# Turning the adjacency in 32x32 squares on VectorE instead of on TensorE

## The chip, the cores and the metric

The kernel runs on one core of one Trainium2 chip. Its time is the device time of one launch in microseconds (us). A core has TensorE (PE; PEld are its weight loads), VectorE (DVE), ScalarE (ACT), GpSimd (POOL) and SyncE (SP), each with its own instruction queue, and 16 DMA engines. SBUF has 128 partitions, PSUM eight banks. Engines wait for one another only by semaphores.

## The reference

A batch of 2048, each with 50 nodes of 32 features. Every sample makes its own two adjacency matrices of 50 x 50, and one gated step is taken with them; what comes behind (batch norm, layer norm, attention pooling over the nodes) is stage three, which the change does not touch.

```python
fusion = x.reshape(b, n * d)                                   # 2048 x 1600
adj = jnp.einsum('bn,tnm->btm', fusion, masker_param) + masker_bias   # 2048 x 2 x 2500
adj = jax.nn.relu(adj).reshape(b, t, n, n)
adj = adj / (adj.sum(axis=-1, keepdims=True) + 1e-06)
m = jnp.einsum('btnd,de->btne', h, weight[i])
m = jnp.einsum('btnm,btmd->btnd', adj, m)
gates = m @ w_ih.T + b_ih + h @ w_hh.T + b_hh
...
```

## The kernel before

The batch lies in 16 tiles of 128 samples. All matrices are fp32; where it matters a value is split into a high and a low part (`_hi`, `_lo`) and a product is made of three.

**Stage one** makes the adjacency. Samples are the partitions of the result; the 5000 columns (2 x 50 rows n of 50 columns m) are cut into 10 groups of 10 rows (`GN`), 500 columns (`GW`). A *window* is one tile and one group: 38 products of 128 x 500 into one of two PSUM banks (`window`, L430; products at L445). Eight windows with the same weights are an *iteration*; 10 iterations are a *block* of eight tiles, and there are two blocks: 160 windows. For each window, one window later:

- ScalarE applies relu from PSUM into `u` (L307).
- VectorE normalises: sum of each row, plus epsilon, reciprocal, product into `an` (`normalise`, L357 to L365).
- TensorE turns `an`, four transposes by a product with the identity, 125 columns each, behind the fourth pair of K blocks of the *next* window (`transposes`, L421, L427, called where `i == T_AT`).
- ScalarE evacuates the turned tile from PSUM into `at` (L313), waiting for the store before last of the same buffer.
- SyncE stores `at` to the scratch `adjT` in HBM (`store_tile`, L201): rows (n, m), columns samples.

In the last window of an iteration ScalarE also casts the next weights to `w_hi` (L288) and VectorE subtracts to `w_lo` (L294); TensorE's first window of the next iteration waits for these. In the first iteration (and the last of block one) the x tiles are split in the same way, one tile a window (L259 to L272); their loads stand in SyncE's queue behind the store of the window before. The order within each engine's queue is written out by hand.

**Stage two** takes tiles one by one, in eight rounds of 16 samples. `load_adj` (L128) brings a tile's adjacency with m in the partitions: 50 partitions for each half of 64 samples, in pieces of 64 samples (256 bytes). `aggregate` (L766) multiplies for each sample its adjacency (moving, 100 columns picked with a step) with its x (stationary), two samples at once for the two halves; then come the gates (L793, L799), the turn of h (on VectorE in 32x32 squares, L708, and on TensorE, L810), and the statistics. SyncE loads a tile's adjacency and x two tiles ahead, when the slot's products are done. The gates of round 6 of an even tile wait for the next tile's three loads (`adj_loaded[1]`, 48 = 3 x 16), behind the products of round 7. The first tile's inputs are loaded in stage one's last iteration; those of the second tile (tile 1) when stage two starts.

Of the kernel before, what the change touches and what calls it, by code (L numbers as in the profile page):

```python
# [17 lines left out]
fp32 = mybir.dt.float32  # L18
# [24 lines left out]
MPAD = 64  # L43
RK = 125
AK = GW // RK
assert AK * RK == GW and AK * P == 512
# [6 lines left out]
T_AT = 3  # L53
# [91 lines left out]
def stage1(nc, place, psum, ins, adjT, shared):  # L145
    xT, W, ident_d = ins["xT"], ins["W"], ins["ident"]
    with ExitStack() as ctx:  # L147
# [9 lines left out]
        ident = sb("ident_sb", [P, P])  # L157
# [6 lines left out]
        x_loaded, ident_loaded = [sem("x_loaded0"), sem("x_loaded1")], sem("ident_loaded")  # L164
# [4 lines left out]
        tr_done, at_ready = sem("tr_done"), sem("at_ready")  # L169
# [8 lines left out]

        def tr_out(c2):

            return psum[0:RK, (2 + c2) * BANK:(3 + c2) * BANK]

# [3 lines left out]
        def _(sp):  # L186
# [25 lines left out]
            sp.dma_start(ident[:, :], ident_d).then_inc(ident_loaded, 16)  # L212
# [89 lines left out]
        def _(act):  # L302
# [17 lines left out]
            for blk in range(BLOCKS):  # L320
                for it, group in p1_iters(act, blk):
                    static = isinstance(it, int)
                    for w in range(BLK):
# [10 lines left out]
                        if split:  # L334
                            for i in range(0, T_AT + 1):
                                split_w_hi(act, i, it + 1)
                        if not (static and it == 0 and w == 0):
                            evacuate(c - 1, (w - 1) % 2, start=static and it == 0 and w <= 2)
                        if split:
                            for i in range(T_AT + 1, NU):  # L340
# [9 lines left out]
            evacuate(c, 1)  # L350
# [1142 lines left out]
```

## Time and profile before

| | us |
|---|---|
| median of 3 runs (lowest, highest) | 2220.93 (2220.83, 2222.51) |
| profiled execution, its own time | 2223.07 |
| span in the profile, first to last instruction | 2221.3 |
| PE busy / DVE busy / ACT busy in the span | 2167.1 / 1088.7 / 956.7 |
| mean granted clock of TensorE, of full speed | 0.988 |
| DMA packets, bytes; packets under 512 B | 341777, 264.48 MB; 169340 |

How to read the rows below. In a windows view each row is a stretch: its length, then for each engine the busy time and the number of instructions, then the granted clock of TensorE (1.00 is 2.4 GHz, 0.50 is 1.2 GHz), the mean busy share of the 16 DMA engines and the GB/s that they moved. In a timeline each row is one instruction or a run of like ones: start, duration, engine, line, output and inputs, count (x16), and in brackets the idle time before it and who ended it. Durations of matmuls overlap, so their pace is read from starts. SPq rows are DMA issues: the duration is how long the issue held the queue, not the transfer.

### The profile page before, as it was taken

The numbers are of one execution on the slowest core, as the hardware profiler recorded it, in microseconds if no ns is written. First come the engines' busy times: TensorE is split into PE (matmuls) and PEld (weight loads), VectorE is DVE, ScalarE is ACT, GpSimd is POOL, SyncE is SP. The second block draws the span as 40 slices with busy tenths as digits, with TensorE's granted clock in tenths as the row PEclk, the third lists the DMA queues.
The fourth block names the chain that finished last, engine by engine and source line by source line (L and its number), as shares of the span: only waits on it lengthen the run. The fifth ranks groups of instructions, "written<-read, shape, count | busy, mean of one in ns | idle before, by whom it ended". The sixth has DMA issues, their size and how long they took to land. (4 is left out here: it accounts for less than half of the span.)

```text
span 2221.3 us, 34738 instructions
## 1 busy us (share of the span) xinstructions
PE 2167.1 (98%) x12334; PEld 1721.3 (77%) x12334; DVE 1088.7 (49%) x2209; ACT 956.7 (43%) x1631; POOL 67.3 (3%) x68
## 2 busy tenths in 40 slices
PE   8999999999999999999999999989999999996898
PEld 7888888888888888888888888867777777775333
DVE  4432233323333433233322333238888888888667
ACT  4321222212223322122221222158888888895862
POOL 0000000000000000000000000010101111010000
PEclk9999999999999999999999999989999999998999
DMA  6412222122205321222212221457776676774660
GB/s 220 157 43 77 92 92 82 41 93 92 92 28 193 125 95 37 85 92 92 74 48 95 92 91 29 118 125 185 189 204 177 193 194 184 197 205 152 191 183 8
DMA packets 341777, 264.48 MB, mean 119 GB/s; under 512 B 169340, under 2 KB 303004, under 8 KB 339996
## 3 DMA queue, kind: packets, MB, share of 16 engines
q1 hardware_dynamic: 323580, 226.12, 34.7%
q10 hardware_dynamic: 18144, 37.69, 5.2%
q8 instruction: 29, 0.48, 0.1%
q14 instruction: 24, 0.20, 0.0%
HBM read 196.08 MB, written 67.70 MB: 119 GB/s over the span
## 5 line engine op out<-in xcount | busy, mean ns | idle before, releaser
L445 PE MATMUL psum<-w_hi,x_lo 128*128 128x500 f32 x2080 | 821.0, 395 | 8.0 <-DVE w_lo L294 8.0
L445 PE MATMUL psum<-w_lo,x_hi 128*128 128x500 f32 (+1 forms) x2080 | 808.3, 389 | 0.0
L445 PE MATMUL psum<-w_hi,x_hi 128*128 128x500 f32 x1920 | 744.0, 388 | 0.0
L357 DVE TENSOR_REDUCE rows<-u 128x10 f32<-128x500 f32 x160 | 107.5, 672 | 887.0 <-ACT u L307 886.4
L445 PEld LDWEIGHTS psum<-w_hi,x_lo 128*128 128x128 f32 x2080 | 391.5, 188 | 82.3 <-issue 8.0
L445 PEld LDWEIGHTS psum<-w_lo,x_hi 128*128 128x128 f32 (+1 forms) x2080 | 391.9, 188 | 72.2
L445 PEld LDWEIGHTS psum<-w_hi,x_hi 128*128 128x128 f32 x1920 | 360.9, 188 | 73.0
L313 ACT COPY at<-psum 125x512 f32<-125x512 f32 x160 | 93.5, 584 | 676.6 <-PE psum L427 676.6
L307 ACT ACTIVATE u<-psum 128x500 f32<-128x500 f32 x160 | 93.8, 586 | 341.3 <-PE psum L445 341.3
L766 PE MATMUL psum<-adj_sb,xs_sb 100*64 100x100 f32 x2048 | 200.6, 350 | 1.6 <-PEq L147 1.6
L766 PEld LDWEIGHTS psum<-adj_sb,xs_sb 100*64 100x64 f32 x2048 | 144.4, 149 | 45.6 <-issue 35.3
L629 ACT ACTIVATE r_gate<-psum,bias 64x400 f32<-64x400 f32 x256 | 151.0, 590 | 22.9 <-PE psum L793 20.8
L288 ACT CAST w_hi<-w_raw 128x1000 fp32r<-128x1000 f32 (+1 forms) x140 | 136.1, 972 | 46.0 <-PE psum L445 44.5
L294 DVE TENSOR_TENSOR w_lo<-w_raw,w_hi 128x1000 fp32r<-128x1000 f32 x120 | 144.0, 1200 | 23.6 <-ACT w_hi L288 15.9
L634 ACT ACTIVATE psum<-psum,bias 64x400 f32<-64x400 f32 x256 | 142.3, 556 | 14.0 <-DVE hG L689 7.1
L746 POOL TENSOR_TENSOR xg_lo<-xg_sb,xg_hi 128x400 fp32r<-128x400 f32 x64 | 67.1, 1051 | 1926.3 <-ACT xg_hi L595 1926.3
L365 DVE TENSOR_TENSOR an<-u,rows 128x500 f32<-128x500 f32 x160 | 108.6, 679 | 6.9
L697 DVE BATCH_NORM_STATS2 stats<-hC 128x128 f32 (+1 forms) x400 | 88.4, 282 | 47.1 <-ACT hC L607 46.6
L427 PEld LDWEIGHTS psum<-ident_sb,an 128*125 128x125 f32 x640 | 94.9, 188 | 16.4 <-DVE an L365 3.0
L427 PE MATMUL psum<-ident_sb,an 128*125 128x128 f32 x640 | 96.5, 274 | 3.4 <-DVE an L365 3.4
L674 DVE SCALAR_TENSOR_TENSOR n_in<-psum,bias,r_gate 128x400 f32<-128x400 f32 x128 | 79.5, 621 | 14.1 <-PE psum L799 13.6
L1127 DVE SCALAR_TENSOR_TENSOR pr<-h,nmu_sb,psum 128x512 f32<-128x512 f32 x100 | 70.0, 742 | 27.9 <-PE psum L1308 26.7
(169 smaller groups left out, 2135.1 us busy)
## 6 DMA issues: line engine op xcount, KB each, us to landing
w_raw<-W SPq DMA_DIRECT2D x140, 500.0 KB, 7.9
adjT<-at SPq DMA_DIRECT2D x160, 250.0 KB
adj_sb<-adjT SPq DMA_DIRECT2D x32, 1250.0 KB
xs_sb<-xz SPq DMA_DIRECT2D x16, 1600.0 KB
hF<-hC ACTq DMA_DIRECT2D x96, 256.0 KB, 6.3
h<-hF SPq DMA_DIRECT2D x64, 256.0 KB, 4.2
xg_sb<-xg ACTq DMA_DIRECT2D x14, 800.0 KB, 8.0
h<-hF SPq DMA_DIRECT2D x48, 192.0 KB, 3.4
```

The costliest lines, as they stand in the source:

```text
L288: nc.scalar.copy(w_hi[:, k0:k1, :], w_raw[:, k0:k1, :]).then_inc(w_hi_ready, 1)
L294: nc.vector.tensor_tensor(w_lo[:, k0:k1, :], w_raw[:, k0:k1, :], w_hi[:, k0:k1, :].bitcast(fp32), ALU.subtract).then_inc(w_ready, 1)
L307: nc.scalar.activation(u[:, c2].rearrange("p n m -> p (n m)"), mm_out(c2), ACT.Relu).then_inc(u_ready, 1)
L313: nc.scalar.copy(at[:, c2].rearrange("p k b -> p (k b)"), tr_out(c2)).then_inc(at_ready, 1)
L357: nc.vector.tensor_reduce(rows[:, 0], u[:, c2], AX.X, ALU.add).then_inc(dve_step, 1)
L365: nc.vector.tensor_tensor(an[:, c2], u[:, c2], rows[:, 2].unsqueeze(2).to_broadcast([P, GN, N]), ALU.mult).then_inc(an_ready, 1)
L427: last = nc.tensor.transpose(tr_out(c2)[:, k * P:(k + 1) * P], flat[:, k * RK:(k + 1) * RK], ident[:, :])
L445: last = nc.tensor.matmul(mm_out(w % 2), a[0:r, w, k, :], b[0:r, k, :], start=k == 0 and n == 0, stop=k == KF and n == 1)
L629: last = nc.scalar.activation(r_gate[half], rz_bank(pair)[half], ACT.Sigmoid, bias=bias[half, R_G:R_G + 1])
L634: last = nc.scalar.activation(z_bank[half], rz_bank(pair)[other], ACT.Sigmoid, bias=bias[other, Z_G:Z_G + 1])
L697: last = nc.vector.bn_stats(stats[:, bass.ds(tile, 1), c, :].rearrange("p i v -> p (i v)"), hC[:, c, :])
L766: last = nc.tensor.matmul(out_[SH * i:SH * i + SH, :, gi], xs[r][:, b, :], adj[r][:, :, b], start=True, stop=True)
```

## The change

VectorE turns each normalised tile right behind `normalise` with one transpose instruction that turns every square of 32 x 32 by itself. `an` becomes one buffer with each row of 50 padded to 64 (`MPAD`), the padding cleared once at the start; `at` holds, in partition 32i+m', for k (m = 32k + m') and n, the 32 samples of group i. The next normalisation waits for the turn of the one before; the turn waits for the store two windows back. TensorE's transposes, ScalarE's evacuation, the identity's load and two PSUM banks go from stage one. The scratch has the order `[tile, k, (i m'), n, s]`, 3.28 MB a tile instead of 2.56; a store is 128 partitions x 2 pieces of 1280 bytes. A tile is loaded in four transfers instead of two, for each half one of the 32 rows with k=0 and one of the 18 rows left, in pieces of 100 x 32 words (12.8 KB); the waits for them go from 48 to 80. The products of `aggregate` pick their moving columns with a step of 32 words instead of 64.

```diff
 def load_adj(sp, shared, adjT, tile, r=0):
     for half in range(2):
-        sp.dma_start(shared.adj[r][N * half:N * half + N], adjT[tile, :, SH * half:SH * half + SH].rearrange("(c m) s -> m c s", m=N)
-                     ).then_inc(shared.adj_loaded[r], 16)
+        for k in range(MB):
+            m0, m1 = TB * k, min(TB * k + TB, N)
+            sp.dma_start(shared.adj[r][N * half + m0:N * half + m1].rearrange("p i c s -> p i (c s)"),
+                         adjT[tile, k, SH * half:SH * half + SH].rearrange("(i m) c s -> m i (c s)", m=TB)[0:m1 - m0]
+                         ).then_inc(shared.adj_loaded[r], 16)
...
-        an = sb("an", [P, 2, GN, N])
+        an = sb("an", [P, GN, MPAD])
-        at = sb("at", [RK, 2, AK, P])
+        at = sb("at", [P, 2, MB, GN, TB])
...
-                sp.dma_start(adjT[tile, bass.ds(group * GW, GW), :].rearrange("(k p) b -> p k b", p=RK),
-                             at[:, c2]).then_inc(at_stored[c2], 16)
+                sp.dma_start(adjT[tile, :, :, bass.ds(group * GN, GN), :].rearrange("k p n s -> p k (n s)"),
+                             at[:, c2].rearrange("p k n s -> p k (n s)")).then_inc(at_stored[c2], 16)
...
-            def evacuate(c, c2, start=False):
-                act.wait_ge(tr_done, c + 1)
-                if not start:
-                    act.wait_ge(at_stored[c2], 8 * (c - c2))
-                nc.scalar.copy(at[:, c2].rearrange("p k b -> p (k b)"), tr_out(c2)).then_inc(at_ready, 1)
...
+            def turn_squares(c, c2, start=False):
+                dve.wait_ge(an_ready, c + 1)
+                if start:
+                    dve.wait_ge(an_cleared, 1)
+                else:
+                    dve.wait_ge(at_stored[c2], 8 * (c - c2))
+                nc.vector.transpose(at[:, c2], an[:].rearrange("p n (k s) -> p k n s", s=TB)).then_inc(at_ready, 1)
...
+            nc.vector.memset(an[:, :, N:MPAD], 0.0).then_inc(an_cleared, 1)
...
                         if not (static and it == 0 and w == 0):
-                            normalise(c - 1, (w - 1) % 2, start=static and it == 0 and w <= 2)
+                            normalise(c - 1, (w - 1) % 2, first=static and it == 0 and w == 1)
+                            turn_squares(c - 1, (w - 1) % 2, start=static and it == 0 and w <= 2)
...
-            def transposes(c, c2, start=False):
-                pe.wait_ge(an_ready, c + 1)
-                if not start:
-                    pe.wait_ge(at_ready, c - 1)
-                flat = an[:, c2].rearrange("p n m -> p (n m)")
-                for k in range(AK):
-                    last = nc.tensor.transpose(tr_out(c2)[:, k * P:(k + 1) * P], flat[:, k * RK:(k + 1) * RK], ident[:, :])
-                last.then_inc(tr_done, 1)
...
-                        last = nc.tensor.matmul(out_[SH * i:SH * i + SH, :, gi], xs[r][:, b, :], adj[r][:, :, b], start=True, stop=True)
+                        last = nc.tensor.matmul(out_[SH * i:SH * i + SH, :, gi], xs[r][:, b, :], adj[r][:, i, :, q * QB + gi], start=True, stop=True)
...
-                    pe.wait_ge(adj_loaded[1], (it + 1) * 48)
+                    pe.wait_ge(adj_loaded[1], (it + 1) * 80)
...
-    adjT = nc.dram_tensor("adjT", [TILES, TN * N, P], fp32, kind="Internal").ap()
+    adjT = nc.dram_tensor("adjT", [TILES, MB, P, TN, TB], fp32, kind="Internal").ap()
```

## Rows read from the trace of the kernel before

**Rows 1.** Windows by stage: length; PE, PEld, DVE, ACT, POOL busy; clock, DMA share, GB/s.
```profile
8.00:1455.00 1447.00, 1446.07 (x6718) 1213.17 (x6718) 466.06 (x849) 355.02 (x539) 0.00 (x0) 1.00 0.27 90
1460.20:2015.00 554.80, 549.65 (x4627) 435.95 (x4628) 466.92 (x1043) 480.35 (x914) 67.08 (x64) 0.99 0.72 190
2015.00:2221.00 206.00, 170.18 (x988) 71.22 (x986) 151.51 (x312) 115.66 (x172) 0.00 (x0) 0.92 0.43 129
```

**Rows 2.** Groups by line: busy us, mean ns of one, idle before it, releaser.
```profile
L427 PE MATMUL psum<-ident_sb,an 128*125 128x128 f32 x640 | 96.5, 274 | 3.4 <-DVE an L365 3.4
...
L708 DVE STREAM_TRANSPOSE hT<-hG 128x800 f32<-128x800 f32 x64 | 64.0, 1004 | 1.7
```

**Rows 3.** TensorE's timeline over one window of stage one: start us, duration us.
```profile
701.01 0.60 PE L427 MATMUL psum<-ident_sb,an 128*125 128x128 f32 x4
701.36 0.48 PE L445 MATMUL psum<-w_hi,x_lo 128*128 128x500 f32 x1
701.67 0.39 PE L445 MATMUL psum<-w_lo,x_hi 128*128 128x500 f32 x1
...
709.80 0.39 PE L445 MATMUL psum<-w_hi,x_hi 128*128 128x500 f32 x1
710.02 0.60 PE L427 MATMUL psum<-ident_sb,an 128*125 128x128 f32 x4
```

**Rows 4.** TensorE's timeline at the change of blocks.
```profile
738.65 0.70 PE L427 MATMUL psum<-ident_sb,an 128*125 128x128 f32 x4 [0.82 <-DVE an L365]
```

**Rows 5.** Timelines of TensorE and VectorE in the last window of an iteration.
```profile
1157.17 0.39 PE L445 MATMUL psum<-w_hi,x_lo 128*128 128x500 f32 x1
...
1159.79 2.55 DVE L294 TENSOR_TENSOR w_lo<-w_raw,w_hi 128x1000 fp32r<-128x1000 f32 x2
...
1166.19 0.39 PE L445 MATMUL psum<-w_hi,x_lo 128*128 128x500 f32 x1
```

**Rows 6.** Timelines of SyncE's queue, VectorE and TensorE in the first iteration.
```profile
63.41 1.12 SPq L192 DMA_DIRECT2D x_raw<-xT  x2
...
70.73 1.83 DVE L269 TENSOR_TENSOR x_lo<-x_raw,x_hi 128x1024 fp32r<-128x1024 f32 x2 [3.67 <-ACT x_hi L259]
...
73.41 0.39 PE L445 MATMUL psum<-w_hi,x_lo 128*128 128x500 f32 x1
```

**Rows 7.** Timeline at the end of stage one and the start of stage two.
```profile
1456.71 0.68 DVE L365 TENSOR_TENSOR an<-u,rows 128x500 f32<-128x500 f32 x1
...
1457.45 1.11 PE L427 MATMUL psum<-ident_sb,an 128*125 128x128 f32 x4 [2.56 <-DVE an L365]
...
1458.59 0.58 ACT L313 COPY at<-psum 125x512 f32<-125x512 f32 x1 [3.08 <-PE psum L427]
...
1460.15 2.97 PE L766 MATMUL psum<-adj_sb,xs_sb 100*64 100x100 f32 x32 [1.59 <-PEq L147]
```

**Rows 8.** Windows with one kind of transfer: adjacency, x tile, store.
```profile
1391.00:1411.00 20.00, 20.00 (x95) 16.78 (x94) 7.55 (x35) 2.93 (x5) 0.00 (x0) 1.00 0.68 144
1417.00:1425.00 8.00, 8.00 (x40) 6.72 (x39) 2.35 (x5) 0.89 (x2) 0.00 (x0) 1.00 0.62 177
1156.00:1158.00 2.00, 2.00 (x10) 1.66 (x10) 0.01 (x1) 0.59 (x1) 0.00 (x0) 1.00 0.33 93
```

**Rows 9.** TensorE's timeline in stage two, adjacency products of rounds 6 to 8.
```profile
1484.73 1.57 PE L766 MATMUL psum<-adj_sb,xs_sb 100*64 100x100 f32 x16
...
1488.79 1.57 PE L766 MATMUL psum<-adj_sb,xs_sb 100*64 100x100 f32 x16
...
1498.70 1.57 PE L766 MATMUL psum<-adj_sb,xs_sb 100*64 100x100 f32 x16
```

**Rows 10.** Window around the wait in tile 0.
```profile
1490.00:1495.00 5.00, 1.20 (x12) 0.87 (x7) 2.20 (x4) 1.29 (x3) 1.03 (x1) 0.67 0.64 164
```

**Rows 11.** SyncE's queue at the start of stage two: start, us of issue.
```profile
1460.84 13.45 SPq L131 DMA_DIRECT2D adj_sb<-adjT  x2
1474.33 7.24 SPq L137 DMA_DIRECT2D xs_sb<-xz  x1
```

More of the change, by code:

```diff
@@ L42 @@
 ITERS = BLOCKS * GROUPS
[L43 to L46, printed above, removed]
+TB = 32
+MB = -(-N // TB)
+MPAD = MB * TB
 SH = P // 2
@@ L52 @@
 NU = len(UNITS)
-T_AT = 3
 XH = 8
@@ L145, in stage1 @@
 def stage1(nc, place, psum, ins, adjT, shared):
-    xT, W, ident_d = ins["xT"], ins["W"], ins["ident"]
+    xT, W = ins["xT"], ins["W"]
     with ExitStack() as ctx:
@@ L168, in stage1 @@
         mm_done, u_ready, an_ready = sem("mm_done"), sem("u_ready"), sem("an_ready")
-        tr_done, at_ready = sem("tr_done"), sem("at_ready")
+        an_cleared, at_ready = sem("an_cleared"), sem("at_ready")
         at_stored = shared.at_stored
@@ L334, in _ @@
                         if split:
[L335 to L340, printed above, removed]
+                            for i in range(NU):
                                 split_w_hi(act, i, it + 1)
@@ L349, in _, with normalise @@
             relu(c, 1)
-            evacuate(c, 1)
         @block.vector
         def _(dve):
-            def normalise(c, c2, start=False):
+            def normalise(c, c2, first=False):
                 dve.wait_ge(u_ready, c + 1)
@@ L362, in normalise @@
                 dve.wait_ge(dve_step, 3 * c + 3)
-                if not start:
-                    dve.wait_ge(tr_done, c - 1)
-                nc.vector.tensor_tensor(an[:, c2], u[:, c2], rows[:, 2].unsqueeze(2).to_broadcast([P, GN, N]),
+                if not first:
+                    dve.wait_ge(at_ready, c)
+                nc.vector.tensor_tensor(an[:, :, 0:N], u[:, c2], rows[:, 2].unsqueeze(2).to_broadcast([P, GN, N]),
                                         ALU.mult).then_inc(an_ready, 1)
+            def turn_squares(c, c2, start=False):
[5 more added lines that the diff above has]
+                nc.vector.transpose(at[:, c2], an[:].rearrange("p n (k s) -> p k n s", s=TB)).then_inc(at_ready, 1)
             def weight_blocks(dve):
@@ L417, in _, with window @@
             normalise(ITERS * BLK - 1, 1)
+            turn_squares(ITERS * BLK - 1, 1)
         @block.tensor
         def _(pe):
-            def transposes(c, c2, start=False):
-                pe.wait_ge(an_ready, c + 1)
-                if not start:
-                    pe.wait_ge(at_ready, c - 1)
-                flat = an[:, c2].rearrange("p n m -> p (n m)")
-                for k in range(AK):
-                    last = nc.tensor.transpose(tr_out(c2)[:, k * P:(k + 1) * P], flat[:, k * RK:(k + 1) * RK], ident[:, :])
-                last.then_inc(tr_done, 1)
-            def window(it, w, blk, c, start=False, bank_free=False, none_before=False):
+            def window(it, w, blk, c, bank_free=False):
                 pe.wait_ge(x_ready, 2 * (blk * BLK + w) + 1)
@@ L450, in window @@
                         last.then_inc(w_used, 1)
-                    if none_before and i == NU - 1:
-                        pe.wait_ge(ident_loaded, 16)
-                    if i == T_AT and not none_before:
-                        transposes(c - 1, (w - 1) % 2, start=start)
             for blk in range(BLOCKS):
@@ L463, in _ @@
                         c = it * BLK + w
-                        window(it, w, blk, c, start=static and it == 0 and w <= 2,
-                               bank_free=static and it == 0 and w < 2, none_before=static and it == 0 and w == 0)
-            transposes(ITERS * BLK - 1, 1)
+                        window(it, w, blk, c, bank_free=static and it == 0 and w < 2)
 def p1_iters(eng, blk):
@@ L818, in turn @@
                     gates(it, s, more)
-            pe.wait_ge(adj_loaded[0], 48)
+            pe.wait_ge(adj_loaded[0], 80)
             aggregate(0)
```

10 lines of the change are left out of this document (3 added, 7 removed).

## The prediction, made before the changed kernel was run

> **What bounds the kernel now.** I read the views in this order: the windows by stage, the costliest groups, then timelines at the places that the change touches. The windows [rows 1] show that stage one (8 to 1455 us) is TensorE alone: busy 1446.07 of 1447.00 us at a granted clock of 1.00, while VectorE has 466.06 and ScalarE 355.02. Stage two (1460.2 to 2015) has three engines near full and the DMA at 0.72 of its engines; stage three is not touched. So in stage one every slot that leaves TensorE's queue is worth its whole length, and up to 981 us of idle VectorE can be spent, as long as no single hand-over becomes late.
>
> **1. The turns leave TensorE.** Each window issues 38 products and one group of four turns. The mean duration of a matmul is no price, since they overlap: [rows 2] give 640 turns of 96.5 us busy in all, but what counts is by how much they shift the next starts. In [rows 3] the turns start at 701.01, the product behind them at 701.36, but that one is longer, so I take the next: 701.67. From 701.67 to the next group of turns at 710.02 are 37 product starts, 8.35/37 = 0.2257 us each. A window is 9.01 us; without turns it is 38 x 0.2257 = 8.577 us; the slot is worth 0.433 us. Groups in the loops: 159 (160 tiles, the last one's lies behind the last product). 159 x 0.433 = **68.9 us**. Its bounds: by the busy time 96.5/160 = 0.60 us each, 96 us, which counts overlap as if it were cost; below, by the shift of the very next start, 0.35 - 0.23 = 0.12 us each, 20 us, which leaves out that this product runs 0.48 instead of 0.39 us. The two starts on either side of a whole window can't be wrong by more than 0.02 us, so 66 to 72 is what I keep.
>
> **2. One stall goes with them.** At the change of blocks TensorE waited 0.82 us for `an` [rows 4], since VectorE had splits of x ahead of the normalisation. No instruction of TensorE waits for `an` any more: **0.8 us**.
>
> **3. What VectorE gets.** One turn of 640 elements a row per window, 160 in all. Nearest row: the turns of 800 elements in stage two, 1004 ns [rows 2]; in proportion 0.80 us; as a fixed cost at most 1.0. I take 0.84 us, between the two and nearer the first; 134 us in all, a rise from 466 to 600 of 1378 us. What is queued behind a turn is, in seven windows of eight, nothing until the next relu, about 5 us later. In the last window of each iteration the new weights' low halves are behind it, and TensorE waits for those. [rows 5]: that window starts at 1157.17, the first two low halves run from 1159.79 as one piece of 2.55, the first ready at 1161.0; TensorE's next iteration starts with them at 1166.19, and without turns it would be 1165.76. The turn moves 1161.0 to 1161.85: 3.9 us in hand. The later pieces come every 1.20 to 1.35 us and TensorE needs one every 6 x 0.2257 = 1.35, so the margin does not shrink. Cost 0; the turn would have to take 4.7 us for the first stall. The wait for the second last store, moved from ScalarE to VectorE, is on a store that was issued about 17 us earlier. Clearing the padding is in VectorE's first 5 us, before the first x has been cast. The store itself is on SP's queue as before, earlier in the window by the 2 us that the turn no longer waits for the fourth unit.
>
> In the first iteration x comes a tile a window, and its margin is thin: the load goes out at 63.41, right behind a store, the low half is made from 70.73 and would be ready at about 72, 1.5 us before its window [rows 6]. In the old chain the store stood behind the evacuation, which stood behind the casts of x, and the next load stood behind the store: a period of 9.1 us. Now the store is due earlier, from VectorE, and the chain is load to low half, 72.0 - 63.4 = 8.6 us, equal to the new window. I book 0; if each of seven windows comes 0.43 late it is 3 us.
>
> ScalarE loses 160 evacuations of 0.58 us; it waited for TensorE in this stage, so 0. The identity's load leaves SP's start; nothing waits behind it that TensorE needs: 0.
>
> **4. The end of stage one.** [rows 7]: `an` is done at 1457.39; the four turns start at 1457.45 and the evacuation ends at 1459.17; then the last store goes out and stage two starts (first product 1460.15). 1.78 us from `an` to `at` become one turn of 0.84 plus a hand-over of 0.04: **0.9 us**.
>
> **5. The loads in stage two.** Per tile 2.56 MB of adjacency, before as 10,000 pieces of 256 bytes, now as 200 rows of 12.8 KB. The first of them alone: [rows 8] 20 us at 144 GB/s with 0.68 of 16 engines, 13.2 GB/s an engine. The x tile in rows of 16 KB: 177 GB/s at 0.62, 17.8 GB/s an engine. In the steady state this hides: TensorE is idle for 5.15 of 554.80 us of the stage [rows 1], and one wait makes most of that. It is in tile 0: the gate for tile 1's inputs is reached behind the products of round 7 at about 1490.3, and TensorE goes on at 1494.16; round starts are 1484.73, 1488.79 and 1498.70 [rows 9], so a round of 4.06 takes 9.91: the wait, and products at a lower clock behind it (0.67 in the mean of 1490 to 1495, [rows 10]). If tile 1 lands before 1490.3 that is **5.8 us**. Landing before: issue of the adjacency at 1460.84, of x at 1474.33 [rows 11]; `xg` just ahead (0.82 MB on 16 engines at 17.8 GB/s, 3 us), then 20 and 9: 32 us, as seen. After, at the x tile's rate per engine: the transfers of 32 rows on 16 engines 1.64 MB / 285 = 5.8 us, those of 18 rows on 9 (below) 0.92 MB / 160 = 5.8 us: 3 + 11.6 + 9 = 24 us, landing near 1485 with 5 us to spare. The other end is no gain in rate at all, 20 us, and the stall stays: 0 of 5.8. The x tile is the nearest row in length, so I take all of it.
>
> How many engines a transfer gets is the unknown. Of the rows here the store of 125 rows holds 0.33 x 16 = 5.3 [rows 8], the loads of 50 and 100 rows about 10: divisors of the row counts, 5 and 10. By this 18 rows give 9. The Trainium skill (DMA: Bandwidth & Descriptors, Why a DMA increments its semaphore by 16 and not by 1) states it as a rule: the largest number up to 16 that divides the slowest dimension of both sides. By that rule, too, it is 9; the trace agrees on 5 and 10.
>
> A rule that speaks against the new loads is in the Trainium skill (SBUF — State Buffer, Door 1: The DMA port swizzle): a transfer into 32 partitions reaches half of the ports, 189 GB/s at 1 MiB, and one into 16 gets 104. By its figures the estimate is 8.7 + 8.9 = 17.6 us instead of 11.6, landing at 1490.5, and the stall is just gone or just there. No row here has a transfer into so few partitions, and the sum goes by the rows.
>
> **6. The products that read it.** The moving operand's step goes from 64 to 32 words, the 1024 products (2048 records) stay. No row shows a dependence on the step; the product's records are alike in all rounds (16 in 1.57 us [rows 9]). I take 0. From both sides: 10% of 1.5 us in 128 rounds is 19 us if TensorE sets every round, either way. Against it: at stage two's start 32 of them take 2.97 us [rows 7], as many a microsecond as later (16 in 1.57), though other products there run at half pace: what sets them is not how fast columns are read.
>
> **Sum.** 68.9 + 0.8 + 0.9 + 5.8 = 76.4 us. The profiled execution took 2223.07 us (span 2221.3): 2146.7. The runs' median is 2220.93, 2.1 below it: 2144.5.
>
> **The rivals.** (a) The stall in tile 0 stays, wholly or mostly, because the short transfers of 18 rows are slow or the last to land: 70.6 off, 2150. For it: the margin is 5 us at the x tile's rate and gone if the adjacency takes 17 us, which lies between the ends of step 5. Chance 0.18. (b) Stage one gets a new bound, above all x's supply in the first iteration or one late hand-over per iteration (VectorE's turn, the weights): 3 us for the first, 20 x 0.3 to 20 x 0.8 for the second, so 2147 to 2160. Against it: the 3.9 us in hand. Chance 0.09. (c) Stage two gets faster by the smaller step or by quieter DMA, 5 to 19 us: 2126 to 2140. For it: DMA at 0.72; against it: the waits there are between engines. Chance 0.06; the same to the slow side 0.04. (d) Slower than before: the transfers of 18 rows get one or two engines instead of nine. At 17.8 GB/s an engine, 0.92 MB on two take 26 us; with 5.8 for the other rows, 9 for x, 3 for `xg` and about 6 for h the tile needs 50 us and has 554.8/16 = 34.7 [rows 1]: 15 us a tile on 14 tiles, 210 us, some 2355. It decides from three engines down (17 us, 41 a tile, 88 us: the gain is gone). Against it: the store and loads above, which got 5 and 10. Chance 0.05, of which 0.01 for three engines, no change. That the change doesn't do what it says (turns still on TensorE) I hold for out of the question by the diff.
>
> **How the numbers follow.** The forecast's case has 0.58: 2144.5. Its own range, from 66 to 72 for the turns and 0.5 for the tail, is 2141 to 2148. To leave out no more than 2 in 10 the range takes (a) and most of (b) and (c): 2134 to 2158. Faster by over 0.2% (4.4 us, about what a measurement of this kernel can tell from no change) are all cases but (d): 0.95, within 0.2% 0.01, slower 0.04.
>
> **What would show it.** Right: windows of 8.58 us from one iteration's start to the next over eight; 600 us of VectorE in stage one with its turns near 0.84 us; stage one's last product near 1385; no wait of TensorE behind round 7 of tile 0 and rounds of 4.06 there; the groups of 256-byte pieces gone from the packets' count; DMA share in stage two below 0.72. Wrong: TensorE waiting for `w_lo` or `x_lo` in stage one; a wait on loads in tile 0 or in later tiles; turns over 1.0 us; the 16 adjacency products over 1.6 us. If the range is missed, it is by step 5 or 6, not by step 1.

## The result, and the profile of the changed kernel

The changed kernel takes 2255.56 us (median of 4 runs, 2254.87 to 2255.84) against 2221.72 for the kernel before on the same chip: ratio 1.0151, 95% interval [1.0133, 1.0168]. It is 34 us slower; the prediction was 2144.5, faster, range 2134 to 2158. The profiled execution took 2254.87 us, its span is 2253.1, where the kernel before has 2223.07 and 2221.3.

The windows by stage of the kernel after, to be read beside [rows 1] (length; busy time of PE, PEld, DVE, ACT, POOL; clock, DMA share, GB/s):

```profile
8.00:1380.00 1372.00, 1371.78 (x6073) 1140.79 (x6074) 592.74 (x1009) 264.48 (x379) 0.00 (x0) 1.00 0.29 103
1386.70:2050.00 663.30, 599.60 (x4663) 470.03 (x4664) 475.69 (x1052) 484.34 (x921) 66.53 (x64) 0.93 0.62 160
2050.00:2253.00 203.00, 167.63 (x951) 68.02 (x949) 147.78 (x303) 112.17 (x165) 0.00 (x0) 0.92 0.43 130
```

Stage one is still TensorE alone, at full clock, with VectorE up by 127 us. Stage two had 5 us of idle TensorE in 555 and now has 64 in 663, and its clock is 0.93. Stage by stage, from the first adjacency product to the first of the last round (1460.15 and 2020.63 before, 1386.72 and 2051.30 after): stage one ends **73.4 us sooner**, stage two is **104.1 us longer** (664.6 instead of 560.5), the rest 1.1 longer. -73.4 + 104.1 + 1.1 = 31.8, the difference of the spans.

The groups of instructions of the kernel after (busy us, mean ns of one | idle time before, and what ended it), first VectorE's new turn and its old one [rows 2], then TensorE's adjacency products and the gate products behind them:

```profile
L358 DVE STREAM_TRANSPOSE at<-an 128x640 f32<-128x640 f32 x160 | 135.3, 846 | 13.3
L688 DVE STREAM_TRANSPOSE hT<-hG 128x800 f32<-128x800 f32 x64 | 64.0, 1004 | 3.8 <-DVE hG L669 2.9
...
L746 PE MATMUL psum<-adj_sb,xs_sb 100*64 100x100 f32 x2048 | 222.6, 375 | 4.4 <-PEq L148 4.4
...
L773 PE MATMUL psum<-m_hi,wd_lo 64*128 64x400 f32 x256 | 60.4, 467 | 64.4 <-DVE m_lo L644 36.8 <-ACT psum L614 24.2 <-issue 3.4
```

The last line holds most of the loss: the gate products waited 64.4 us. The waits of the kernel after in stage two, ScalarE's and VectorE's views (us in total, times, longest), say for what the two releasers waited themselves:

```profile
ACT xg_hi L575 <- DMA xg_sb<-xg: 34.0, 8, 5.7
...
DVE m_lo L644 <- issue: 38.8, 5, 8.1
```

I read the starts of TensorE's 128 rounds in both timelines and subtracted each from the next. Before, rounds take 4.46 us with turns on TensorE and about 4.1 without, but for round 7 of tile 0. After, three things are new:

- every undisturbed round is 0.1 to 0.2 longer (4.57 to 4.70, and 4.24 to 4.29): about 20 us in all;
- five rounds of 13.6 to 14.5 us, each at the point where a dynamic loop (two tiles an iteration) jumps back: 46.7 us over the normal;
- eight rounds of 8.2 to 11.6 us, in which ScalarE waited for `xg`: 38.6 us over the normal.

A stall costs more than its wait. In the round that begins at 1639.67 TensorE waits 7.10 us, and the round is 9.3 us longer than a normal one. While TensorE stands, its granted clock falls to 0.50, and it is back at 1.00 only about 5 us after the products go on; until then pairs of gate products start 0.33 us apart instead of 0.18. Three stretches of that round and the next in the kernel after (columns as above):

```profile
1643.00:1645.00 2.00, 0.00 (x0) 0.00 (x0) 0.00 (x0) 0.00 (x0) 0.00 (x0) 0.50 0.58 126
1649.00:1651.00 2.00, 2.00 (x13) 1.52 (x10) 1.38 (x3) 1.10 (x3) 0.00 (x0) 0.50 0.78 241
1655.00:1657.00 2.00, 2.00 (x21) 1.55 (x18) 1.93 (x6) 1.01 (x3) 0.00 (x0) 1.00 0.53 201
```

Of the 104 us that stage two grew by, 59 are more idle time of TensorE and about 20 are the longer rounds; the rest, some 25 us by subtraction (an estimate), is work at the lower clock behind the waits.

One of the five rounds at the jump, in VectorE's timeline of the kernel after (the last turn of an iteration, the first instruction of the next), and the same place in the kernel before:

```profile
1639.15 1.01 DVE L688 STREAM_TRANSPOSE hT<-hG 128x800 f32<-128x800 f32 x1
1647.86 0.57 DVE L644 TENSOR_TENSOR m_lo<-psum,m_hi 128x400 fp32r<-128x400 f32 x1 [7.69 <-issue]
```

```profile
1647.23 1.01 DVE L708 STREAM_TRANSPOSE hT<-hG 128x800 f32<-128x800 f32 x1
1648.16 0.54 DVE L664 TENSOR_TENSOR m_lo<-psum,m_hi 128x400 fp32r<-128x400 f32 x1
```

"issue" means that the engine waited for no semaphore. It had no instruction. The DMA view, window 1640 to 1940, has 19 packets on an instruction queue (packets, MB, share), each of 8 KB; they come as VectorE and ScalarE move on in their programs:

```profile
q14 instruction: 19, 0.16, 0.2%
```

In the same window of the kernel before there is none on that queue; in the whole span it has 24, the kernel after 50. (A second instruction queue, q8, has packets of 16 KB. None of its packets recurs with the jumps: in that window it has one in the kernel before and none in the kernel after.) And of the transfers that ScalarE issues, from issue to landing, first before and then after:

```profile
xg_sb<-xg ACTq DMA_DIRECT2D x8, 800.0 KB, 8.0
hF<-hC ACTq DMA_DIRECT2D x8, 64.0 KB, 4.4
```

```profile
xg_sb<-xg ACTq DMA_DIRECT2D x6, 800.0 KB, 14.3
hF<-hC ACTq DMA_DIRECT2D x7, 64.0 KB, 19.8
```

### The profile page after: what moved, and what is told of

It is laid out like the page before. It is cut to its first block and busy times, and to the rows that moved or that the text cites. A ratio compares the mean times of both kernels' runs of the same rounds, so it can differ in the third digit from the quotient of the medians.

```text
span 2253.1 us, 33249 instructions
## 1 busy us (share of the span) xinstructions
PE 2141.4 (95%) x11694; PEld 1680.5 (75%) x11694; DVE 1221.3 (54%) x2370; ACT 866.1 (38%) x1471; POOL 66.7 (3%) x68
## 5 line engine op out<-in xcount | busy, mean ns | idle before, releaser
L431 PE MATMUL psum<-w_hi,x_lo 128*128 128x500 f32 x2080 | 806.3, 388 | 8.2 <-DVE w_lo L289 8.2
L746 PE MATMUL psum<-adj_sb,xs_sb 100*64 100x100 f32 x2048 | 222.6, 375 | 4.4 <-PEq L148 4.4
L746 PEld LDWEIGHTS psum<-adj_sb,xs_sb 100*64 100x64 f32 x2048 | 154.7, 153 | 55.8 <-issue 39.4
L358 DVE STREAM_TRANSPOSE at<-an 128x640 f32<-128x640 f32 x160 | 135.3, 846 | 13.3
L289 DVE TENSOR_TENSOR w_lo<-w_raw,w_hi 128x1000 fp32r<-128x1000 f32 x120 | 137.7, 1190 | 3.7 <-ACT w_hi L283 2.2
L773 PE MATMUL psum<-m_hi,wd_lo 64*128 64x400 f32 x256 | 60.4, 467 | 64.4 <-DVE m_lo L644 36.8
L773 PEld LDWEIGHTS psum<-m_hi,wd_lo 64*128 64x128 f32 x256 | 25.2, 191 | 108.0 <-issue 66.6
L644 DVE TENSOR_TENSOR m_lo<-psum,m_hi 128x400 fp32r<-128x400 f32 x128 | 70.7, 553 | 43.3 <-issue 38.8
```

What stands on the lines that cost most here:

```text
L289: nc.vector.tensor_tensor(w_lo[:, k0:k1, :], w_raw[:, k0:k1, :], w_hi[:, k0:k1, :].bitcast(fp32), ALU.subtract).then_inc(w_ready, 1)
L358: nc.vector.transpose(at[:, c2], an[:].rearrange("p n (k s) -> p k n s", s=TB)).then_inc(at_ready, 1)
L431: last = nc.tensor.matmul(mm_out(w % 2), a[0:r, w, k, :], b[0:r, k, :], start=k == 0 and n == 0, stop=k == KF and n == 1)
L746: last = nc.tensor.matmul(out_[SH * i:SH * i + SH, :, gi], xs[r][:, b, :], adj[r][:, i, :, q * QB + gi], start=True, stop=True)
L773: last = nc.tensor.matmul(rz_bank(pair), w[half], m[half], start=first, stop=final)
```

## The experiments

Each ratio is to the kernel before, run beside it on the same chip, with its 95% interval. The diffs are shortened: what sets semaphores, and lines that only follow from an edit, are left out.

### The four parts taken apart

**x1**: VectorE's turn kept, the scratch in an order that the old loads can read.

```diff
-                sp.dma_start(adjT[tile, :, :, bass.ds(group * GN, GN), :].rearrange("k p n s -> p k (n s)"),
-                             at[:, c2].rearrange("p k n s -> p k (n s)"))
+                for i in range(P // TB):
+                    for k in range(MB):
+                        m0, m1 = TB * k, min(TB * k + TB, N)
+                        sp.dma_start(adjT[tile, m0:m1, bass.ds(group * GN, GN), TB * i:TB * i + TB],
+                                     at[TB * i:TB * i + m1 - m0, c2, k])
...
+        sp.dma_start(shared.adj[r][N * half:N * half + N], adjT[tile, :, :, SH * half:SH * half + SH])
```

The loads are of 256-byte pieces again and the products step by 64 words.

> VectorE's turn and stage one as in the changed kernel, but the scratch lies as [tile, m, n, sample]: stores in pieces of 128 bytes (8 transfers a window), loads in stage two as before (two of 50 rows, pieces of 256 bytes, step 64). Theory L (the whole loss comes from the form of the loads and the step of the products that read them): stage one ends near 1382 us, stage two takes its old 555 us without waits at the loops' edges: 2145 to 2155 us. Rival S (the turn on VectorE or the way stage one hands over leaves stage two slower): as the changed kernel, about 2255. If the small stores are a price of their own it shows as waits in stage one, up to 2170.

2192.95 us, 0.9877 [0.9861, 0.9894]: far above theory L's 2145 to 2155, so L is not the whole. The rounds are 4.46 again and no wait for `xg` is left, but five rounds of 12.4 to 13.2 us stay at the jump. So these come neither from the loads nor from the step. The small stores have a price too: stage two starts at 1390.57, 3.8 us later than in the kernel after.

**x2**: the kernel after, each adjacency load cut in ten along n.

```diff
+            for c0 in range(0, TN, GN):
-                sp.dma_start(shared.adj[r][N * half + m0:N * half + m1], adjT[tile, k, SH * half:SH * half + SH] ...)
+                sp.dma_start(shared.adj[r][N * half + m0:N * half + m1, :, c0:c0 + GN],
+                             adjT[tile, k, SH * half:SH * half + SH, c0:c0 + GN] ...)
```

Its pieces are 1280 bytes instead of 12.8 KB.

> The changed kernel with each adjacency load cut along n into ten (40 transfers a tile, pieces of 1280 bytes instead of 12.8 KB; same rows 32 and 18, same places in SBUF). Theory P (long pieces hold the DMA engines, and xg, h and the loops' instructions wait behind them): the waits of 3 and 8 us per pair of tiles go, about 14 x 7 = 85 to 100 us off: 2160 to 2175 us. Rival Q (32 and 18 rows reach few ports or few engines, whatever the pieces): the waits stay, 2240 to 2260.

2180.5 us, 0.9808 [0.9792, 0.9825], 5 us above the range of theory P. The waits for `xg` are gone (landing 5.5 us), the five rounds at the jump are 6.4 to 7.9 instead of 14, the step's part stays. That the row counts of 32 and 18 are to blame for the waits is out: they are as in the kernel after.

**x3**: the kernel before with the products reading at a step of 32 words (other elements of the same rows, so the values are others).

```diff
-  adj[r][:, :, b]
+  adj[r] as (i c s), s = 32: [:, i, :, q * QB + gi]
```

> The kernel before with one edit: the adjacency products read their 100 moving columns with a step of 32 words instead of 64 (so they multiply the wrong columns of the same tile; the rest is as before). Theory D (the step alone makes the 16 products longer, 1.72 instead of 1.57 us): 128 x 0.13 to 0.15 = 17 to 19 us slower, 2238 to 2241. Rival (the products are longer in the changed kernel because of DMA traffic or the clock): no change, 2221.

2242.88 us, 1.0091 [1.0074, 1.0108], 21.1 us more than before and 2 above the range, no new stall (only round 7 of tile 0 is long, 8.5, as before), and rounds with turns of 4.57 to 4.70 from the first to the last. TensorE's timeline of x3, one group of 16 products, where [rows 9] has 1.57 for it:

```profile
1629.56 1.77 PE L766 MATMUL psum<-adj_sb,xs_sb 100*64 100x100 f32 x16
```

and the group of all of them, with the mean of 375 ns that the kernel after has too (x1 and the kernel before, at step 64: 350):

```profile
L766 PE MATMUL psum<-adj_sb,xs_sb 100*64 100x100 f32 x2048 | 222.1, 375 | 1.6 <-PEq L147 1.6
```

**x4**: the kernel after with step 64 in the products (again other elements).

```diff
-  adj[r][:, i, :, q * QB + gi]
+  adj[r] as (n s), s = SH: [:, :, b]
```

> The changed kernel with one edit: the products read their columns with the old step of 64 words (the wrong columns of the same tile). Theory D: products of 1.57 us again, 15 to 20 us off where TensorE sets the round, 2235 to 2245. Rival: 2255 as the changed kernel, the products stay at 1.72.

2248.55 us, 1.0119 [1.0102, 1.0136]: only 7 us back, not the 10 to 20 expected. The rounds are 4.46, but the stalls grow (nine waits for `xg`, rounds up to 12.5). What is taken from a round comes back as a wait while the transfers set the pace.

### The jump: where VectorE's loop lies

The trace lets one count instructions. VectorE's loop of stage two has 289. Counting each loop body once, it begins at instruction 590 before and at 688 after: the turn adds two instructions to every window that is written out, 98 in all. In x2, instruction packets come when VectorE is at these places:

```
us into the span   1582.8  1614.2  1619.4         1622.1  1628.1  1658.7  1690.9
VectorE is at         833     960     976 (jump)     692     715     833     963
```

So it is fed in stretches of 128 instructions with edges at 704, 832 and 960, one packet of 8 KB each, and twice more at the jump (at 976 and at 692). Before, the loop 590 to 878 lies in three stretches (576 to 960). After, 688 to 976 lies in four. The theory F: in three it stays in the engine, in four its beginning has been displaced when VectorE jumps back, and it waits for a new fetch. The test moves the loop and nothing else, by small memsets in the 4.7 us in which VectorE waits for the first loads:

```diff
+            for i in range(32):                        # x5, x8; 8 in x6; 96 in x7 (there into `an`)
+                nc.vector.memset(pad[:, i:i + 1], 0.0)
```

> VectorE's turn with the old scratch order and loads, as x1, and 32 small memsets more on VectorE before its first work (in the 4.7 us in which it waits for the first loads). Counted from the trace, VectorE's loop of stage two has 289 instructions; it begins at instruction 590 in the kernel before and at 688 in the kernel after and in x1. In the trace of x2 the instruction queue's packets come each time VectorE passes 704, 832 and 960 (steps of 128) and at its jump back. Theory F (place in the stream): the loop lies in three stretches of 128 in the kernel before (576 to 960) and in four in x1 and after (576 to 1088), and only in four it is fetched anew at every jump. Here it begins at 720 and ends at 1008, three stretches again: the five stalls at the jump go (rounds about 4.5 instead of 12.4 to 13.2), about 24 to 28 packets on the instruction queue instead of 53, and the time is 2145 to 2158 us. Rival T (the stall comes from the turn or from what the faster stage one leaves behind, or the program's length decides): the five stalls stay, the time stays at 2190 to 2198 us.

> As x5 with 8 small memsets instead of 32. The loop begins at 696 and still lies in four stretches of 128. Theory F: nothing changes against x1, 2189 to 2198 us, five rounds of 12 to 13 us, about 53 packets. Rival A (any shift, or the memsets themselves, takes the stall away): as x5.

> The kernel before with 96 small memsets on VectorE before its first work. The loop of stage two begins at 686 instead of 590 and then lies in four stretches of 128. Theory F: five rounds of 12 to 13 us appear where the kernel before has 4.5, 50 packets or more on the instruction queue instead of 24, and the time rises by 38 to 44 us to 2259 to 2266 (up to 3 us of it from the memsets themselves, which may outlast the wait for the first loads). Rival T: the time rises by 0 to 3 us alone and no round of stage two changes.

> The kernel after with the 32 memsets alone; its loads, its step and its scratch are as they are. Theory F: the five stalls at the jump (rounds of 13.6 to 14.5 us) go, the waits for xg_sb (rounds of 8 to 12 us) stay, and the time falls by about 47 us to 2203 to 2214. Rival: both kinds of stall have one cause, the long transfers, so the time at the jump only moves to waits for xg_sb or stays: 2240 to 2256.

| kernel | loop begins | stretches | instruction packets | rounds at the jump | us, median | ratio |
|---|---|---|---|---|---|---|
| before | 590 | 3 | 24 | 4.5 | 2223.2 | 1 |
| x7, before + 96 | 686 | 4 | 50 | 12.9 to 13.1 | 2264.27 | 1.0186 [1.0169, 1.0203] |
| x1 | 688 | 4 | 53 | 12.4 to 13.2 | 2192.95 | 0.9877 [0.9861, 0.9894] |
| x6, x1 + 8 | 696 | 4 | 53 | 10.1 to 12.2, the next 4.7 to 9.0 | 2194.58 | 0.9868 [0.9851, 0.9884] |
| x5, x1 + 32 | 720 | 3 | 28 | 4.5 | 2149.76 | 0.9679 [0.9662, 0.9695] |
| x8, after + 32 | 720 | 3 | 24 | 4.6 | 2233.24 | 1.0050 [1.0033, 1.0067] |

F's forecast holds in both directions: 32 memsets make x1 43 us faster, 8 do nothing, and 96 make the kernel before 41 us slower, without any part of the change in it. What this shows is that the place of VectorE's loop decides. Why it does, that a fourth stretch displaces the first, is argued and not shown: the fast kernels begin their loop 14 and 16 instructions behind an edge, the slow ones 110 to 120, and nothing between was tried, nor a loop of another length. VectorE's timeline of x7 at a jump has what the kernel after has:

```profile
1690.73 1.01 DVE L710 STREAM_TRANSPOSE hT<-hG 128x800 f32<-128x800 f32 x1
1698.38 0.57 DVE L666 TENSOR_TENSOR m_lo<-psum,m_hi 128x400 fp32r<-128x400 f32 x1 [6.64 <-issue]
```

x8 is a miss in size: the five stalls went, as F says, but the time fell by 22 us and not by 47, into neither of the two ranges. (Its profiled execution, which the next line is from, was its fastest, 2223.96; the others took 2231 to 2236.) The waits for `xg` took part of their place, as x8's view of ScalarE's waits shows against 34.0 us in 8 above:

```profile
ACT xg_hi L578 <- DMA xg_sb<-xg: 55.7, 13, 6.2
```

### The waits for xg: which pieces hold it up

Over all kernels, ScalarE waited for `xg` each time that it took 16.9 us or more to land, and never when it took 15.4 or less. I took the adjacency's 12.8 KB pieces for the cause (x2). Three runs on top of the 32 memsets put that to the test.

```diff
 x9:  + sp.wait_ge(xg_loaded[r], (it + 2) * 16)    # ahead of the adjacency and xs of tile t+2
 x10: x2 + 32 memsets
 x11: + for c0 in range(0, TN, TN // 2):           # each adjacency load in two, 6.4 KB pieces
```

> x8 (the kernel after with the 32 memsets) and one wait more on SyncE: the adjacency and xs of tile t+2 are issued only when xg of tile t+2 has landed, a round after the point at which they were issued before. Theory Q (the 12.8 KB pieces, queued at once on all engines just ahead of xg, hold xg up: it lands after 18.4 us in x8 instead of 8.0 in the kernel before): xg lands in 5 to 9 us, the 13 rounds of 6 to 12 us with ScalarE waiting for xg_sb go, rounds 4.57 to 4.70, and the time falls from 2233 to 2168 to 2180. Rival R (xg is late for its own reason, its buffer or the memory it reads, or the adjacency, begun a round later, now comes late itself): waits of the same size stay, on xg_sb or on the adjacency, and the time stays above 2200.

> x2 (each adjacency load cut in ten, pieces of 1280 B, step 32 words) with the 32 memsets. Theory F: the five rounds of 6.4 to 7.9 us at the jump fall to about 4.6, some 13 to 16 us in all, and the time from 2180 to 2164 to 2170; the step's 20 us stays. Rival: nothing at the jump is left to gain once the pieces are short, and as in x8 a wait for a transfer takes its place: 2176 to 2184.

> x8 with each adjacency load cut in two (pieces of 6.4 KB instead of 12.8). Theory Q, delay of xg in proportion to the piece: xg lands in 11 to 14 us instead of 18.4 (1280 B: 5.5), the waits for xg_sb shrink to under 2 us each, 2170 to 2190. Rival: it is the number of bytes queued ahead of xg, not the length of a piece (the bytes are the same in both): xg lands at 17 to 19 us and the time stays at 2222 to 2236.

x10 came as F has it: 2166.76 us, 0.9751 [0.9735, 0.9768], no stall but tile 0's. The other two missed. x11 took 2246.59, 1.0106 [1.0089, 1.0123]: half the piece, and `xg` still lands in 19.4 us. x9 took 2323.37, 1.0453 [1.0435, 1.0470]: `xg` lands in 4.4 us and nobody waits for it, but now TensorE waits for the loads themselves, once a tile. TensorE's waits in x9, and SyncE's queue there:

```profile
PE psum L777 <- DMA xs_sb<-xz: 105.9, 12, 9.9
```

```profile
1724.04 1.79 SPq L131 DMA_DIRECT2D adj_sb<-adjT  x4
1726.01 0.30 SPq L138 DMA_DIRECT2D xs_sb<-xz  x1
```

Issued at 1724.04, the last of their packets end at about 1751, 27 us later, and a tile has 36. `xg` itself is issued about 13 us behind the point at which x8 issues the loads (1635.1 and 1622.1) and lands in 4.4; 13 + 4.4 + 27 is more than 36. The loads have no room for a start that waits for `xg`.

Then I read SyncE's queue (start, us of issue) in the kernel before, in the kernel after and in x2, in this order:

```profile
1601.01 9.72 SPq L131 DMA_DIRECT2D adj_sb<-adjT  x2
1610.92 8.68 SPq L137 DMA_DIRECT2D xs_sb<-xz  x1
```

```profile
1628.37 1.93 SPq L131 DMA_DIRECT2D adj_sb<-adjT  x4
1630.48 0.30 SPq L138 DMA_DIRECT2D xs_sb<-xz  x1
```

```profile
1607.39 20.71 SPq L132 DMA_DIRECT2D adj_sb<-adjT  x40
1628.28 0.83 SPq L139 DMA_DIRECT2D xs_sb<-xz  x1
```

Thousands of 256 B pieces kept SyncE's queue busy for 9.7 us, and `xs` with its 16 KB pieces is issued 9.9 us behind the adjacency; with whole rows it is 2.1 us. When the pieces move says more than when they are issued. In the kernel before `xs` begins at 1622.6, right behind the adjacency's last pieces, and `xg`, issued at 1614.4 among the 256 B pieces, has landed at 1622.5. In x8, one tile: adjacency issued at 1622.1, `xg` at 1635.1, `xs` in bulk from 1639, and more than half of `xg`'s bytes move only from 1649 on, when `xs` is nearly done. Theory S: `xs` is what holds `xg` up. Three runs, one edit each:

```diff
 x12 (on x8):  load_adj(...)
              + sp.wait_ge(xg_loaded[r], (it + 2) * 16)
                load_xs(...)
 x13 (on x8): + for b in range(0, 64, 8):           # xs in eight transfers of 2 KB pieces
 x14 (on x10): load_xs ahead of load_adj
```

> x8 (the kernel after, VectorE's loop back in three stretches) with one wait more on SyncE, behind the adjacency's four transfers and ahead of xs: xs is issued only when xg of the same tile has landed. What x11 and x9 showed: halving the adjacency's pieces changes nothing in xg's landing (19.5 against 18.4 us), and holding adjacency and xs back both brings it to 4.4. Theory S: the pieces that hold xg up are xs's of 16 KB, which the kernel after queues 2 us after the adjacency's issue begins, where the kernel before and x5 queue them 9 us after it and x10 20 us after it (a load of many short pieces keeps SyncE's queue busy); xg's 2 KB pieces take turns with them one by one. Then xg lands in 8 to 12 us, the 13 waits for xg_sb mostly go, and the time is 2170 to 2195. Rival Q (the 12.8 KB pieces of the adjacency hold it up as well): xg lands later than 14 us, and the time stays above 2210.

> x8 with xs in eight transfers of 2 KB pieces, issued where it is issued in x8. Theory S with the length of the piece deciding: behind the adjacency's long pieces xg's 2 KB pieces now take turns with xs's 2 KB, xg lands in 10 to 14 us and the time is 2175 to 2205. Rival (bytes queued ahead decide, whatever their pieces): xg lands at 17 to 20 us, 2220 to 2236. Rival Q expects this too, from the adjacency's pieces alone.

> x10 (adjacency in 1280 B pieces, no stall left, 2166.8 us) with xs issued ahead of the adjacency instead of behind it. Theory S: xs's 16 KB pieces now stand in the queues when xg is issued, xg lands in 10 us or later instead of 5.3, and if over 14 us, waits for xg_sb come back; 2170 to 2200. Rival Q (only the adjacency's pieces matter): xg lands in 5 to 7 us as in x10 and the time stays at 2165 to 2170.

`xg`'s own pieces, which the expectations of x12 and x13 take for 2 KB, are 6.4 KB: 128 packets of 6400 bytes in the trace.

| kernel | adjacency's pieces | xs's pieces, issue after the adjacency's | xg lands | us, median | ratio |
|---|---|---|---|---|---|
| x8 | 12.8 KB | 16 KB, 2 us | 18.4 us | 2233.24 | 1.0050 [1.0033, 1.0067] |
| x11 | 6.4 KB | 16 KB, 4 us | 19.4 | 2246.59 | 1.0106 [1.0089, 1.0123] |
| x12 | 12.8 KB | 16 KB, 20 us | 7.3 | 2166.88 | 0.9751 [0.9734, 0.9767] |
| x13 | 12.8 KB | 2 KB, from 2 us | 10.2 | 2164.60 | 0.9744 [0.9728, 0.9761] |
| x14 | 1280 B | 16 KB, ahead | 10.2 | 2166.68 | 0.9749 [0.9732, 0.9765] |
| x10 | 1280 B | 16 KB, 20 us | 5.3 | 2166.76 | 0.9751 [0.9735, 0.9768] |

From the DMA views, x8 and x12:

```profile
xg_sb<-xg ACTq DMA_DIRECT2D x7, 800.0 KB, 18.4
```

```profile
xg_sb<-xg ACTq DMA_DIRECT2D x7, 800.0 KB, 7.3
```

and SyncE's queue in x12, `xs` 20 us behind the adjacency and the next tile's adjacency 16 us behind that:

```profile
1601.33 1.93 SPq L131 DMA_DIRECT2D adj_sb<-adjT  x4
1621.35 0.30 SPq L138 DMA_DIRECT2D xs_sb<-xz  x1
1637.75 1.80 SPq L131 DMA_DIRECT2D adj_sb<-adjT  x4
```

Holding back `xs` alone takes all 13 waits away, and so does cutting its pieces where it stands. x12 and x13 did better than expected (2170 and 2175 at the least). In x13 the issue of `xs` took 8 to 14 us instead of 0.3, but its pieces move when x8's do: in the tile whose `xs` is issued at 1600.8, nine tenths of them from 16.3 to 26.8 us behind the issue, in x8 (1503.2) from 16.1 to 26.7, with `xg` issued about 11 us behind it in both. So between these two the length of `xs`'s pieces is what differs, and with it how much of `xg` moves beside them. The DMA view of 7 us of x8 (1642 to 1649) and of 4 us of x13 (1617 to 1621), both inside the stretch in which `xs` and `xg` are under way together; q1 has SyncE's transfers, q10 ScalarE's, `xg` and the stores of h (packets, MB, share of the engines). Of q10's bytes `xg`'s packets have 0.06 MB in x8 and 0.56 in x13:

```profile
q1 hardware_dynamic: 73, 1.16, 55.1%
q10 hardware_dynamic: 221, 0.33, 14.7%
```

```profile
q10 hardware_dynamic: 220, 0.69, 50.2%
q1 hardware_dynamic: 193, 0.36, 28.6%
```

x14 missed: `xg` lands in 10.2 us, as S says, but no wait came and the time was the rival's. It is also a weak test, for `xs` is nearly through (14.1 to 16.3 us behind its issue) when `xg` is issued, 13.0 us behind it. So the 12.8 KB pieces without `xs` beside them can be borne (x12), and with `xs` in 16 KB pieces they can't (x8); `xs`'s 16 KB pieces fully beside `xg` with a short-pieced adjacency were not tried. That halving the adjacency's pieces alone changes nothing is x11.

**x15**, the version the runs point to, x5 with its transfers spread over more engines:

```diff
+        for m0, m1 in ((0, 48), (48, N)):     # adjacency; xs as 0:96 and 96:100
```

> x5 (2149.8 us) with each transfer of 50 rows cut in 48 and 2 and xs's 100 rows in 96 and 4. The count of the 4-byte packets in a load's window says that a transfer of 50 or 100 rows is on 10 engines and one of 32 on 16; 48 and 96 are to be on 16. The loads of a tile end earlier (in x5 31 us after the first issue), and the one stall that x5 has left, round 7 of tile 0 (7.12 instead of 4.1 us), shrinks: 2145 to 2150. Rival: the small transfers hold SyncE's queue or the engines 0 and 1, nothing changes or a stall comes: 2149 to 2160.

2150.04 us, 0.9674 [0.9658, 0.9690]: the same as x5, at the meeting of both ranges, which decides nothing. Round 7 of tile 0 fell from 7.13 to 4.76 and stage two is 1.9 us shorter (556.5 against 558.4), but in the profiled executions it begins 0.4 later and what follows it is 2.5 longer. The DMA share of stage two rose from 0.70 to 0.94 at the same 189 GB/s: the engines are busy a third longer with the same bytes, and tile 1's inputs are complete 30.8 us behind the start of stage two instead of 31.5. x5's stage two, by its window, is again what [rows 1] had before:

```profile
1389.50:1947.90 558.40, 554.99 (x4670) 440.20 (x4670) 471.70 (x1053) 485.73 (x923) 67.03 (x64) 0.99 0.70 189
```

## Why the prediction was wrong, step by step

**Steps 1 and 2, the turns leave TensorE: right.** A window went from 9.01 to 8.57 us (products of the kernel after at 704.89 and 713.46), and stage two starts 73.4 us sooner, where steps 1, 2 and 4 have 70.6. The other 2.8 us I have not taken apart.

**Step 3, VectorE's turn: right in its price, wrong in what it left out.** 846 ns against 0.84, no late hand-over in stage one. But "cost 0" counted time alone. The turn also makes VectorE's program longer, and that moved its loop of stage two over an edge: 46.7 us in the kernel after, 43 by x1 and x5. No sentence of the prediction looks at the place of code; this is the step with the largest failure, and it alone turns 76 us of gain into 30.

**Step 4: right**, contained in the 73.4.

**Step 5, the loads: wrong.** The text says "in the steady state this hides". The loads' own rate did hide; what they do to the others did not. I priced the adjacency as bytes by a rate and left out who shares the engines: that `xs` would be issued nearly 8 us sooner behind the adjacency, and that `xg` would have to share with the long pieces of both. 38.6 us in the kernel after, 56 once the stalls at the jump no longer hide it. The 5.8 us of tile 0 did not come either: round 7 took 9.75 us against 9.91. SyncE issued the loads at 1387.42; the kernel after's window from 1416 has TensorE standing and the DMA busy still, where [rows 10] has 1490:

```profile
1416.00:1419.00 3.00, 0.17 (x2) 0.00 (x0) 2.20 (x4) 0.94 (x3) 1.03 (x1) 0.77 0.73 165
```

The last piece of tile 1's `xs` ends at 1418.2, 31 us behind the issue of `xg`, where I had 24. Two terms were too short. `xs` takes 12.0 us from issue to last packet where it is loaded by itself (tile 0, in stage one), not 9: the 177 GB/s of [rows 8] had other transfers in them. My 11.6 us for the adjacency was too short as well: tile 0's, issued at 1319.36 in the kernel after with only stage one's stores and weights beside it, ends 16.6 us later, and in x12, where it has `xg` and stores beside it but no `xs`, it takes 17 to 19. Here the estimate by the figures of the Trainium skill (SBUF — State Buffer, Door 1: The DMA port swizzle), which I set aside, had 17.6. No run shows that the ports are the reason, but that estimate was the better one. The gain in tile 0 was there to be had: in x13, with `xs` in 2 KB pieces, tile 1's inputs are complete 28.6 us behind the start of stage two, not 31.4 as in the kernel after, and round 7 takes 4.24. The nine engines were right: the 4-byte packets that end transfers are 60 a tile, 16 + 9 + 16 + 9 for the adjacency and 10 for `xs`.

**Step 6, the products' step: wrong.** I took 0 and wrote the bound beside it: 19 us. x3 shows 21.1. The argument against it was that at the start of stage two 32 of these products go at their usual pace while the others run at half pace (granted clock 0.50). That shows that TensorE's clock does not set them; it says nothing against the reading of the columns, and no row had another step. In x3 the step costs something at that very place, 3.23 us where [rows 7] has 2.97:

```profile
1460.11 3.23 PE L766 MATMUL psum<-adj_sb,xs_sb 100*64 100x100 f32 x32 [1.60 <-PEq L147]
```

Why the smaller step is slower stays open.

**The rivals.** (a) came true and was worth what it said, 5.8. (c) on its slow side, chance 0.04, is x3. (d), the slower one, fell: nine engines, not two. The real loss was in none of them. Taken together, in the profiled executions: 73.4 off, 20 for the step, 46.7 for the jump, 38.6 for `xg`, 1.1 in stage three; that is 33 and the spans differ by 31.8. The 46.7 and the 38.6 include the work at the lower clock behind each wait.

That this sum is not only arithmetic is what x5 shows: turn kept, step and loads as before, the loop in three stretches, 2149.76 us, 73.4 below its kernel before. That this is the same 73.4 is chance: its small stores let stage two start 2.8 us later than in the kernel after (1389.56), and stages two and three, 2.1 and 1.0 us shorter than before, give that back. It also lies in the range that the prediction gave for the change, but it is another kernel, without the new loads. And x12 and x13 are 15 to 17 above it with the step alone left, where the step costs 20.

## What to carry to other kernels

Before a price is put at zero because an engine has time, ask what else the edit moves: its instructions shift every loop behind them, and a loop of some hundred instructions that lay in three stretches can come to lie in four (VectorE's here, 289 instructions). Look for "issue" at a loop's jump and count the instruction packets; a few dead instructions in idle time are the test and the cure. A load of many short pieces can leave room for the transfers of another queue: who makes it leaner should look at what follows it in its queue, and at whose transfer then runs beside long pieces. And price a stall of TensorE by the longer round, not by the wait: here 9.3 us for 7.1.

## What the runs showed of the hardware that I had not expected

- VectorE's instructions come in 8 KB packets of 128. A loop of 289 over three such stretches runs without a fetch; over four it is fetched anew at each of five jumps: 8.5 us a jump beside 256 B pieces (x7), 9.3 beside the long pieces (after), 2.6 beside 1280 B pieces (x2). From one fetch to the next at the jump there are 4 to 5 us in x1. TensorE's loop of 658 instructions is longer by far, and no packets recur at its jumps beyond VectorE's, so what holds for VectorE doesn't hold for it.
- TensorE reads a moving operand of 100 columns more slowly at a step of 32 words than of 64: 375 against 350 ns in the mean of 2048, 0.1 to 0.2 us for 16 products, 21 us in the kernel. The pace at a step of 64 is the same at a granted clock of 0.50 (32 in 2.97 us) and of 1.00 (16 in 1.57).
- With all bytes the same, the landing of another queue's 800 KB in 6.4 KB pieces went from 4.4 us (x9) to 19.4 (x11), depending only on the pieces and the spacing of what SyncE had queued. With the spacing kept and 16 KB pieces cut to 2 KB (x8 and x13) it went from 18.4 to 10.2.
- In the kernel after, TensorE's granted clock fell to 0.50 in each of the five waits at the jump, for 6.8 to 10.2 us with the work behind them in it; the wait of 7.1 us that is shown above made its round 9.3 us longer.
